# Expert stages of a macaron block: each row block is loaded and transposed once and kept, and each visit copies the kept block

## The reference

```
def ffn(x):                                    # x after layernorm
    probs = softmax(x @ router_w)              # 16 experts
    weights, idx = top_k(probs, 2); weights /= weights.sum()
    h = silu(x @ gate_w[e]) * (x @ up_w[e])    # for the two chosen experts e
    return sum of weights * (h @ down_w[e])
x = x + 0.5 * ffn(layernorm(x))
x = x + attention(layernorm(x))                # causal, rotary, 16 heads over 4 kv heads
x = x + 0.5 * ffn(layernorm(x))
```

## Time and profile before

| | before |
|---|---|
| median of 3 runs | 837.42 us (837.4 to 837.98) |
| the profiled execution | 837.85 us |
| its span, first to last instruction | 836.0 us |
| mean granted PE clock | 0.977 |
| busy: PE, DVE, ACT, POOL | 91%, 76%, 70%, 53% of the span |
| first expert stage, first to last gate and up product | 38.75 to 149.09 us |
| second expert stage, the same | 717.62 to 807.96 us |

### The profile page before, as it was taken

The page is one execution under the profiler, slowest core; times in us unless marked ns, Lnnn a source line. Parts: engine busy times, 40 slices in busy tenths (PEclk is TensorE's granted clock), DMA queues, the critical chain, the costliest instruction groups (busy, mean ns, idle before and its releaser), DMA issues.

```text
span 836.0 us, 16221 instructions
## 1 busy us (share of the span) xinstructions
PE 759.8 (91%) x4584; PEld 655.4 (78%) x4584; DVE 637.6 (76%) x1839; ACT 581.1 (70%) x1534; POOL 446.7 (53%) x382
## 2 busy tenths in 40 slices
PE   3698999799999999999999999999999999999980
PEld 2586788687878888888888888889887788789970
DVE  5555675578898888889988989998879888755572
ACT  2365657787777888878778777789777676556640
POOL 1671605587565775665658546374544585003374
PEclk8799999999999999999999999999999999999995
DMA  9498962111000010000001000000000055357785
GB/s 313 129 346 262 282 187 83 64 27 26 1 1 14 14 20 8 1 14 14 1 9 19 2 2 2 1 0 3 7 2 1 20 198 173 113 155 236 209 245 176
DMA packets 52918, 70.63 MB, mean 84 GB/s; under 512 B 7264, under 2 KB 44640, under 8 KB 52448
## 3 DMA queue, kind: packets, MB, share of 16 engines
q1 hardware_dynamic: 40736, 47.54, 18.0%
q0 software_dynamic: 9216, 16.82, 8.2%
q10 hardware_dynamic: 2880, 5.24, 1.9%
HBM read 42.80 MB, written 26.77 MB: 83 GB/s over the span
## 4 chain that ended last, share of the span: by engine, by line
PE 65%; POOL 10%; issue 9%; DVE 8%; DMA 3%; ACT 2%; SPq 1%; DVEq 0%; POOLq 0%; ACTq 0%
PE ps L1698 53%; PE ps L1904 6%; POOL sb_ropeB L1643 2%; POOL sb_xf L1646 2%; PE ps L1757 2%; POOL xs L1604 1%; DVE sb_x L1480 1%; POOL sb_x L1634 1%; POOL xs L1612 1%; DMA sb_wF_raw<-ys,sb_pos 1%; PE ps L1771 1%; DVE sb_prob L1453 1%; PE ps L1718 1%; DVE sb_wF L1460 1%; POOL sb_wF L1654 1%
## 5 line engine op out<-in xcount | busy, mean ns | idle before, releaser
L1698 PE MATMUL ps<-sb_wF 128*128 128x512 f32 (+2 forms) x1056 | 260.0, 373 | 6.3 <-DVE sb_wF L1470 4.9
L1698 PEld LDWEIGHTS ps<-sb_wF 128*128 128x128 f32 x1056 | 171.3, 189 | 25.5 <-issue 5.4
L1643 POOL TENSOR_TENSOR sb_ropeB<-sb_ropeB,sb_sin 128x512 f32<-128x512 f32 x80 | 110.9, 1386 | 104.8 <-ACT sb_ropeB L1004 104.7
L1023 ACT ACTIVATE sb_prob<-sb_prob,sb_nmax 128x128 f32<-128x128 f32 (+3 forms) x256 | 142.1, 559 | 33.3 <-DVE sb_nmax L1453 32.5
L1698 PE MATMUL ps<-sb_wF,sb_wA 128*128 128x512 f32 x576 | 155.1, 404 | 6.0 <-ACT sb_ropeB L1004 5.3
L1654 POOL TENSOR_TENSOR sb_wF<-sb_xf,sb_wF 128x384 fp32r<-128x384 f32 (+1 forms) x75 | 82.3, 1106 | 115.5 <-ACT sb_wF L1016 115.3
L1480 DVE SCALAR_TENSOR_TENSOR sb_x<-ps,sb_rinv,sb_x 128x256 f32<-128x256 f32 x256 | 122.5, 479 | 19.9 <-PE ps L1698 8.8
L1698 PEld LDWEIGHTS ps<-sb_wF,sb_wA 128*128 128x128 f32 x576 | 102.0, 188 | 32.3 <-ACT sb_ropeB L1004 13.7
L1032 ACT ACTIVATE sb_wF<-ps 128x512 fp32r<-128x512 f32 x160 | 95.3, 596 | 43.3 <-PE ps L1904 42.6
L1460 DVE TENSOR_TENSOR sb_wF<-ps,sb_wF 128x512 fp32r<-128x512 f32 x160 | 109.2, 684 | 19.3 <-ACT sb_wF L1032 18.1
L1698 PE MATMUL ps<-sb_wA,sb_wF 128*128 128x256 f32 x768 | 115.5, 286 | 4.0 <-DVE sb_x L1480 3.3
(11 more groups left out here) (177 smaller groups left out, 1263.9 us busy)
## 6 DMA issues: line engine op xcount, KB each, us to landing
ys<-sb_wA_raw SPq DMA_DIRECT2D x124, 128.0 KB, 2.8
sb_wF_raw<-xs SPq DMA_DIRECT2D x44, 128.5 KB, 3.8
sb_wA_raw<-xs SPq DMA_DIRECT2D x44, 128.5 KB, 2.2
sb_work<-xs SPq DMA_DIRECT2D x36, 128.5 KB, 2.9
sb_wA_raw<-in_wattn ACTq DMA_DIRECT2D x18, 256.0 KB, 4.6
sb_wF_raw<-in_wgu SPq DMA_DIRECT2D x4, 768.0 KB, 10.4
sb_wF_raw<-in_wdn SPq DMA_DIRECT2D x4, 768.0 KB, 12.1
sb_wA_raw<-in_wgu SPq DMA_DIRECT2D x4, 768.0 KB, 7.1
```

The costliest lines, as they stand in the source:

```text
L1023: nc.scalar.activation(own, own, ACT.Exp, scale=-1.0, bias=nmax[:, k % 2, h:h + 1], accum_out=ssum[:, k % 2, h:h + 1]).then_inc(exp_done, 1)
L1643: nc.gpsimd.tensor_tensor(ropeB[:, slot], ropeB[:, slot], sin[:], ALU.mult).then_inc(rope_mul, 1)
L1698: return nc.tensor.matmul(out, lhsT, rhs, start=start, stop=stop)
```

## The change

Rows are now loaded by block and not by visit (`load_block`, 64 loads in place of 124, no table read on SP; a ring of six tiles). PE turns each block once (`turn`), DVE copies it from PSUM into a place where it stays for the pool (`keep`; ACT does it for the first two blocks of pool 2), in the first stage with its weight column behind it by a second copy. For each visit ACT copies the kept block of that visit into one of five slots of `xT` (`visit`), from an address that it works out from the table; the first visit of a pool takes block 0. In the second stage the weight column is not kept. ACT gets the table from a row in one partition (`row_tab`), to which SP moves it by a small DMA, and reads it eight values at a time (`read_table`). PE reads its own table value for each visit as before. In DVE's order the block copies stand ahead of the gating product of the step. The first stage's two pools no longer overlap: pool 0's last two down products come before pool 1's first turns. A block is turned four steps ahead of its own first possible visit and copied three steps ahead; two blocks each are turned in the two steps ahead of pools 0 and 1 and in steps 0 and 1 of pool 2. The attention's q slots are used in reverse order and the first mask is loaded later, since kept blocks lie in these places.

```
     def has_tile(q, at):
+        if q.n == 0:
+            return q.tiles <= at < q.end
+        return pools[2].tiles <= at < pools[3].end
...
-        def load_tile(q, s):
-            at = q.tiles + s
...
-            if at >= XR:
-                sp.wait_ge(y_evac, at - XR + 1)
-            sp.dma_start(tile_at(q, at), xs[q.p][bass.ds(e * -P + s * P, P), :]).then_inc(xg_in[at % XR], 16)
+        def load_block(q, r):
+            t = q.at + r
+            if r == 0:
+                sp.wait_ge(scattered[q.p], 16 * q.nt * (1 if q.n == 0 else 2))
+            if t >= XR:
+                sp.wait_ge(xt_kept, t - XR + 1)
+            if q.n == 0 and r == XR:
+                sp.wait_ge(weight_read, q.p + 1)
+            width = RW if q.n == 0 else D
+            sp.dma_start(block_rows(t)[:, 0:width], xs[q.p][r * P:(r + 1) * P, 0:width]).then_inc(xg_in[t % XR], 16)
...
+        def read_table(q, at):
+            if at == 0:
+                act.wait_ge(row_tab_in[q.p], 16)
+            more = min(AT_ONCE, q.ns - at)
...
+        def visit(q, s):
+            at = s - q.tiles
...
+            act.wait_ge(xt_kept, q.at + min(at, q.nr - 1) + 1)
+            if s >= TURNED:
+                act.wait_ge(y_evac, s - TURNED + 1)
+            block = block_of_visit(q, at, visited.pop(s))
+            width = D + 1 if q.n == 0 else D
+            nc.scalar.activation(xT[:, s % TURNED, 0:width], block, ACT.Copy).then_inc(xt_done, 1)
...
-                if has_tile(n, at + 2) and (n == 0 or i + 2 >= AHEAD or q.p == 3):
-                    xt_copy(at + 2)
+                if has_tile(q, at + 2) and (n == 0 or i + 2 >= AHEAD or q.p == 3):
+                    visit(pool_of(at + 2), at + 2)
...
+                ahead = at + 3
+                if has_tile(q, ahead) and (ahead - pool_of(ahead).tiles) % AT_ONCE == 0 and ahead != pools[2].tiles:
+                    read_table(pool_of(ahead), ahead - pool_of(ahead).tiles)
...
+        def keep(q, r):
+            t = q.at + r
+            dve.wait_ge(xt_ps, t + 1)
+            if r == 0 and q.n == 0:
+                dve.wait_ge(xt_done, q.tiles + 1)
+            ins = nc.vector.tensor_copy(kept_block(q, r, D), x_at(t))
+            if q.n == 0:
+                ins = nc.vector.tensor_copy(kept_block(q, r, RW)[:, D:RW], block_rows(t)[:, D:RW])
+            ins.then_inc(xt_kept, 1)
...
-        def tile_transposes(q, s):
-            pe.wait_ge(xg_in[s % XR], loaded(s))
+        def turn(q, r):
+            t = q.at + r
+            pe.wait_ge(xg_in[t % XR], loaded(t))
+            if t >= 2:
+                pe.wait_ge(xt_kept, t if t == pools[2].at + AHEAD else t - 1)
...
-                if has_tile(n, at + 2) and (n == 0 or i + 2 >= AHEAD or q.p == 3):
-                    tile_transposes(pool_of(at + 2), at + 2)
+                for block in turned_blocks(q, at):
+                    turn(*block)
```

More of the change, by code:

```diff
@@ L34, in __init__ @@
         self.ns = self.nr + z.E - 1
-        self.end = tiles + self.ns
+        self.end, self.left = tiles + self.ns, at + self.nr
 class Sizes:
@@ L67, in program @@
         pools.append(Pool(z, len(pools), n, b0, b1, before.end if before else 0,
-                          before.halves + before.nh if before else 0))
+                          before.halves + before.nh if before else 0, before.left if before else 0))
     MT = max(q.nt for q in pools)
     NFIRST = pools[1].end
+    TAB, TURNED, AT_ONCE = max(q.ns for q in pools), 5, 8
     def sb(name, shape, dt, at=ctx):
@@ L718, in steps @@
         first, second = pools[2 * n:2 * n + 2]
+        if n == 0:
+            for q in (first, second):
+                for i in range(-2, q.ns + 2):
+                    yield q, i, q.tiles + i
+            return
         for i in range(-2, first.ns + second.ns + 2):
@@ L826, in mask, with first_tiles, last_tiles @@
             sp.dma_start(mask_slots(n), A["mask"]).then_inc(mask_in[n], 16)
[L828 to L834, removed]
-                    then()
-                due = first.ns - RING if m == first.ns else m - XR + 1
-                while out < due:
-                    store_tile(*loads[out])
-                    out += 1
-                load_tile(q, s)
-            while out < len(loads):
-                store_tile(*loads[out])
-                out += 1
+        def first_tiles():
+            early, late = pools[0:2]
+            for r in range(early.nr):
+                load_block(early, r)
+            for i in range(2, early.ns + 2):
+                if i == 6:
+                    table_row(late)
+                store_tile(early, i - 2)
+                if i == early.ns - RING + 1:
+                    for r in range(XR):
+                        load_block(late, r)
+            for i in range(-2, late.ns + 2):
+                if i >= 2:
+                    store_tile(late, i - 2)
+                for q, r in kept_blocks(late, late.tiles + i):
+                    if r + XR < late.nr:
+                        load_block(late, r + XR)
+                if i == late.nr + E - 4:
+                    sp.wait_ge(xt_done, late.tiles + late.nr + E - 5)
+                    mask(0)
+        def last_tiles(then):
+            early, late = pools[2:4]
+            blocks = [(early, r) for r in range(early.nr)] + [(late, r) for r in range(late.nr)]
+            for r in range(XR):
+                load_block(early, r)
+            n = XR
+            for i in range(late.end - early.tiles + 2):
+                if i >= 2:
+                    q = pool_of(early.tiles + i - 2)
+                    store_tile(q, early.tiles + i - 2 - q.tiles)
+                if i == XR:
+                    then()
+                elif i == early.ns - 12:
+                    table_row(late)
+                while n < len(blocks) and n < i + 3 + XR and (n < early.nr or i >= early.ns - 10 + n - early.nr):
+                    load_block(*blocks[n])
+                    n += 1
         for b in range(B):
@@ L1054, in do @@
                 elif what == "X":
-                    xt_copy(pools[2].tiles + n)
+                    keep(pools[2], n)
+                elif what == "R":
+                    read_table(pools[2], 0)
+                elif what == "Y":
+                    visit(pools[2], pools[2].tiles + n)
                 elif what == "silu":
@@ L1584, in scatter @@
                 pool.wait_ge(to_done, q.p + 1)
-                pool.wait_ge(xt_ps, NFIRST)
+                pool.wait_ge(xt_ps, pools[1].left)
                 pool.wait_ge(xn_done[q.p], q.nt)
@@ L1958, in do @@
                 elif what == "X":
-                    tile_transposes(pools[2], pools[2].tiles + n)
+                    turn(pools[2], n)
                 elif n == 12:
```

164 lines of the change are left out of this document (111 added, 53 removed).

## The result

| | before | changed kernel |
|---|---|---|
| median | 837.41 us (837.18 to 837.98, 4 runs) | 855.2 us (853.61 to 857.41, 4 runs) |
| ratio | | 1.0206, interval 1.0191 to 1.022 |
| profiled execution, its span | 837.85, 836.0 us | 857.41, 855.3 us |
| mean granted PE clock | 0.977 | 0.967 |

The account below looks back on a forecast made before the run. PE was taken to bound the expert stages and POOL's gathers the end. Nine place-by-place terms came to 8.4 us less than 837.85: 829.4, or 829.0 on the median's scale; range 822 to 839 for 8 in 10.

Parts of the forecast that it names:

- The table reads: ACT's eight-word reads, between copy of h and silu: 0.7 us each, fitting into 0.66, costing nothing in the sum.
- the words are read one by one: Rival: reads hold ACT ahead of silu and delay PE's down product; 22 us, 852 at the upper bound; chance 0.20.
- The attention tail: ACT's first read of pool 2's table stands there: +0.7 us, bounds 0 and 2.
- The entry: Entry to the second stage: two extra turns and two block copies ahead of the last residual adds, +0.5 us.
- term 1: Pool 0 and passage to pool 1: 0, since nothing brings the scatters forward; bounds 1 earlier to 3 later.
- Pool 1: Up to step 23: -2.9 us, bounds -8.3 to +1.8; the rest: -1.4, bounds 0 and -2.8.
- the rival had DVE as the bound of the whole: First stage: waits for DVE replace the transposes and pool 1's gains vanish, 833 to 836 us; chance 0.16.
- Pool 2's short steps: In pool 2, 15 short steps save 0.19 us each: -2.9.
- SP's lag: Pool 2's last store, issued late behind SP's loads and register reads, and POOL's first gather come earlier: -1.7 us.
- The gathers' pace: POOL's 31 gather intervals at the end shrink from 1.32 to 1.28 us each: -1.2.
- terms 7 to 9: From pool 2's last result to the last gather: SP's lag -1.7, pool 3's first block +0.5, gathers -1.2; -2.4 us.
- term 8: Pool 3's first block: its scatter has fewer microseconds of visits to hide behind, +0.5 us (0 to 2).

Follow-up runs that it names:

- experiment 1: Changed kernel with the odd pools' table row starting 40 words in instead of 39: 846.41 us, ratio 1.0098.
- Experiment 2: Changed kernel with pool 2's table row issued ahead of the down weights instead of behind them: 851.26 us, ratio 1.0156.
- experiment 4: Changed kernel without table reads on ACT, each visit taking the block of its own number, at most the last: 840.24 us, ratio 1.003.
- experiment 14: Kernel with PE's table read ahead of the transposes and ten blocks on ACT; ACT reads one value at a time instead of eight: 834.4 us, ratio 0.9948.
- experiment 11: Run with ten blocks on ACT, GpSimd instead of DVE taking low halves of eleven weight splits in pool 1: 841.35 us, ratio 1.0021.
- 13: Run with ten blocks on ACT, PE's table read for the next visit moved ahead of a step's transposes: 834.43 us, ratio 0.9946.
- experiment 12: Run with ten blocks on ACT, DVE making two more one-column copies behind each of pool 1's blocks 4 to 23: 836.19 us, ratio 0.9954.
- experiment 7: Changed kernel with twelve more table reads behind ACT's last work, in two lists of starts and counts: 852.66 and 855.03 us.

## Why the prediction was wrong

**The table reads: the step that failed.** I took 0.31 + 7 x 0.055 = 0.7, "because dispatch and address are paid once", and let it cost nothing. Measured were 1.65 us in the median and 10 to 15 us of the kernel's time. The 0.7 is right for six of the 16 reads (0.55 to 0.76). For ten it is wrong: they start off a multiple of four words or take seven; no row of before could show this, since it had only single reads, but TAB = 39 stood in the program, and I priced all reads alike. The rival "the words are read one by one" named the place, and the bound of 1.5 us (the median was 1.65), with a price of 22 at most; that words are read one by one is not shown, only that start and count matter. A rule of the Trainium skill stood beside it (Runtime: NRT & Kernel Launch, section on instruction fetch mechanics), some 200 ns for each register in bulk too; the Trainium skill tells it of loads from HBM, and these come from SBUF. The trace is of that order for full reads off the boundary, 0.24 to 0.41 us for each word behind a first one of 0.28, and not for those on it: 0.04 a word.

**The attention tail (+0.7, got 6.5).** I saw that the row is issued behind the down weights and took the transfer for small. It is small, but lands only after them: ACT's read starts 10.3 us after its issue, 0.75 behind the weights' landing. Bounds of 0 and 2 left that out, though the earlier trace rows puts the weights' issue only 7.5 us ahead of ACT's place. The Trainium skill has the rule (DMA: Bandwidth & Descriptors, section on queues, rings and completion order): on each DMA engine the descriptors of one issuing engine are taken up in ring order. The trace agrees: in the changed kernel and in experiment 1 the read starts 0.75 and 1.1 us behind the weights' landing. Experiment 2 shows that the wait goes with the row ahead of the weights, where the tail lost 0.3 us.

**The entry (+0.5, got 5.66).** I counted two turns and two copies as work and not what they wait for: copies stand in DVE's order behind adds and norm, and PE's turns wait for copies. Moving four copies took 3.2 us off, about half of it low clock. Some 1.6 us stay in the best version.

**The passage (term 1: 0, got 1.77, within its bounds).** From pool 0's last product to pool 1's first it took 7.34 us, and 6.12 without reads (experiment 4): the long read is some 1.2 of it. In eight later executions the first product of pool 1 comes 5.83 to 5.88 us behind the last of pool 0, be that one at 70.3 or at 72.3: there the draining of pool 0 and the copies swallow its gain, and not the scatters that I named. In experiment 14 the first rows had landed at 71.89, and PE turned them at 74.02, behind pool 0's last steps.

**The clock** was no term at all. Five pauses of 1.6 to 4.3 us came with a stretch at half clock, in which PE was busy 18.8 of 20.5 us; that is an estimated 9.4 us of PE time at most. It does not follow every such pause: the one of 2.58 in experiment 1 (up to 732.50) had none.

**Pool 1 (-2.9 and -1.4, got 2.45 and 1.66).** With reads, row and entry mended, and ten blocks on ACT, it is -1.95 and -0.2. Single executions with short reads (experiment 11 aside) vary from -3.1 (experiment 14) to +0.75 (13, with late blocks), so that the first term is right in sign at best. Its reason was partly wrong: I put 3.5 us of stalls to DVE around the norm, and the rival had DVE as the bound of the whole; experiment 12's copies show that it has room. Part of the stalls is likely PE's own table read, which the prediction left as it was. The second term ends at its bound of 0: the long steps there, which hold a projection, take 2.5 to 3.5 us before and 2.7 to 3.7 without turns.

**Pool 2's short steps (-2.9).** Right in kind: 1.26 to 1.27 us, 0.15 less than 1.42 and not 0.19. Without long reads (ten blocks on ACT) the stretch from visit 69 to 101 gave 1.4.

**SP's lag (-1.7).** Misread. The store at 783.36 was that of visit 101; visit 100's is the one at 782.05, 0.5 behind its result. From the end of pool 2's last result to the first gather it took 4.13 before and 3.02 after: 1.1, not 1.7. **The gathers' pace** was right: 1.277 us on average where 1.28 was forecast, without the reads (experiment 4); with them two intervals of 2.40 and 2.73 undid it. In the run with ten blocks on ACT terms 7 to 9 come to -2.6, where -2.4 was forecast. That is luck in part: the lag gave 1.3 there and not 1.7, and the 0.5 that term 8 was to cost does not show.

```profile
803.47 0.99 POOL L1771 DMA_INDIRECT sb_wF_raw<-ys,sb_pos  x1 [18.36 <-DMA ys<-sb_wA_raw]
...
845.92 0.95 POOL L1771 DMA_INDIRECT sb_wF_raw<-ys,sb_pos  x1 [0.31 <-DVE sb_x L1503]
```

So the idea is worth 0.5%, 4 us, once its costs are off the path. Open stay the late blocks in pool 1, the rest at the entry, and the long reads from word 8.

## What to carry to other kernels

Work that is taken off the bounding engine comes back as waits between the others: before a saving is counted, list what each moved instruction waits for and what is queued behind it, on its engine and in its DMA queue. A register read that is grouped to save time has to be measured as it will stand, with its start and its number of words; here it was short only from a multiple of four words and in full groups, and one word at a time was as good. When one number in a program (here a row's length) sets addresses, it is a cost to be looked at like any loop.

## What the runs showed of the hardware

- In the runs of experiment 7, eight words took 0.54 to 0.78 us from a multiple of four words (two reads from word 8 took 1.54 and 1.85), and 1.75 to 4.50 from elsewhere; one word 0.28.
- A table row of 39 values was issued 1.2 us behind the second of two weight transfers of 768 KB each (in the changed kernel). The weights landed at 711.54 and the read of the row started at 712.29, 10.3 us after its issue.
- While GpSimd worked on 128x512 subtractions, two of DVE's operations on 128x4 took 1.19 instead of 0.16 us, and two on 128x256 1.29 each instead of 0.41, while its product and result, which read PSUM, stayed at 0.26 and 0.48 or less. The Trainium skill has a rule that fits (SBUF — State Buffer, section "Who interferes with whom"): the two share a port pair, which one holds for a whole instruction. That gave the norm some 5 us in one run.
- In the changed kernel five of PE's pauses, of 1.6 to 4.3 us, came with 3.4 or 6.8 us at a granted clock of 0.50 (two of these stretches began before the pause was over). A pause of 2.58 us in experiment 1 had none.
